# A graph-attention kernel: no summed table in its prologue, copies dealt to two more engines, and a last stage that adds on TensorE

## The chip, the cores and the metric

One NeuronCore of a Trainium2 chip runs the whole kernel. The metric is the device time of one execution in microseconds (us), less is better. Engines are named as in the profile: PE (TensorE, matrix products), DVE (VectorE), ACT (ScalarE), POOL (GpSimd) and SP (the engine that issues most transfers).

## The reference

One layer of graph attention over N = 6250 nodes with 256 features, 206,250 edges sorted by destination, 8 heads of 16 channels.

```
h    = relu(layernorm(x))
xm   = h @ W_n2m.T;  ea = edge_attr @ W_r2m.T
xl   = xm @ Wl.T + bl;  xr = xm @ Wr.T + br
# each node also gets a loop edge whose attribute is the mean of ea over its edges
u      = leaky_relu(xl[src] + xr[dst] + ea @ We.T, 0.2)
logits = sum over the 16 channels of a head of u * att
alpha  = softmax of logits over the edges of one destination
out    = segment_sum(xl[src] * alpha, dst) + bias
result = x + out @ W_m2n.T
```

## The kernel before

Nodes are cut into 49 windows of 128. The kernel has three stages, one function each, with a barrier between them; nothing of a stage overlaps the next.

**`prologue`** loads x, builds the index tables and masks, multiplies the weight matrices together, and then runs the **projection loop** over the 49 windows. In it, for window w: ACT writes `h` (the normalised and clipped x, L411); PE transposes it in two halves (L483, L484); DVE copies the transpose to `hT` (L647); PE forms `[xl | xr]` in two accumulated products with `Wall` (L490, L491); DVE adds the biases into `lr_sb` (L653). `xr` is then split into three bf16 parts whose sum is the float32 value, kept in `xr_parts`: ACT rounds it (L416), DVE forms the remainder `rest` (L658), ACT rounds that (L421), DVE stores the last remainder (L663). The steps of one window are spread over four turns of the loop. ACT, PE, DVE, POOL and SP each have an instruction list of their own, written out by hand; semaphores tie them. Each of xl and xr carries 8 extra columns (`ROW` = 136), the share of each head's logit that is linear in it (0.2 times the sum with `att`), so the product is 272 columns wide. POOL adds the two halves into `both` (L361) and SP stores it as `both_table` (L308) beside `xl_table` (L306). The extra columns of the weights come from `Watt`, `Wshare` and the copies L606 to L625, and PE spreads the bias row by a product (L473) ahead of the loop.

**`edge_loop`** walks the edges in 427 steps of 512: gathers xl rows by POOL's indirect transfers, adds xl, xr (through `xr_parts` and a one-hot matrix) and edge terms on PE, and gathers weighted sums into `acc`.

**`finale`** goes over the windows in 7 batches of `FB` = 7. For batch n: DVE takes `mean` of the edge attributes; PE transposes it (L1188), ACT copies it to `meanT` (32 rows, L1218), PE multiplies it with `Wc` (L1195); DVE adds `both_in`, loaded from `both_table`, giving `z` (L1290), takes `u_att` = max(z, 0) * att (L1292), sums it per head and adds the 8 linear columns for the loop edge's logit. For the batch b before it: DVE scales the gathered sums and the node's own xl by their weights (`old` L1268, `own` L1273), adds them (`two`, L1279), divides (`gat`, L1284); PE transposes `gat` (L1201), ACT copies it to `gatT` (L1221), PE multiplies it with `W_outT` in two groups of 4 and 3 windows through one buffer (L1209), ACT copies each to `result` (L1230), POOL adds x (L1175), SP stores. Each engine takes batch n = b + 1 and batch b in the same turn. The order on DVE in a turn is: means of n, everything of b up to `gat`, then `z` of n up to the softmax differences `falls`.

Of the kernel before, what the change touches and what calls it, by code (L numbers as in the profile page):

```python
# [24 lines left out]
ROW = D_MSG + HEADS  # L25
# [91 lines left out]
def gat_kernel(nc, x, src, dst, edge_attr, W_n2m, W_r2m, Wl, bl, Wr, br, We, att, bias, W_m2n, out):  # L117
# [6 lines left out]
    both_table = nc.dram_tensor("both_table", (WINDOWS * P, ROW), FP32, kind="Internal").ap()  # L124
# [4 lines left out]
    with ExitStack() as ctx:  # L129
        def sb(name, shape, dt=FP32):  # L130
# [8 lines left out]
        att_relu = sb("att_relu", [P, D_MSG])  # L139
        att_pad = sb("att_pad", [P, 2 * ROWS - HEADS])  # L140
        Wc = sb("Wc", [P, ROW])
# [12 lines left out]
                 both_table, xr_parts, ident, ident16, ones, iota_n, node_of, att_relu, att_pad, Wc, Wc2, W_outT,  # L154
# [6 lines left out]
        finale(nc, banks, x, xl_table, both_table, ident, att_relu, Wc, W_outT, bias_col, acc, out)  # L161


def prologue(nc, banks, xl_table, meta_dram, slot_dram, masks_dram, inputs,
             both_table, xr_parts, ident, ident16, ones, iota_n, node_of, att_relu, att_pad, Wc, Wc2, W_outT,
# [6 lines left out]
    with ExitStack() as ctx:  # L172
# [3 lines left out]
        def sem(name):  # L176
# [3 lines left out]
        lr_sb = sb("lr_sb", [P, WRING, 2 * ROW])  # L180
        lr_bias = sb("lr_bias", [P, 2 * ROW])
        rest = sb("rest", [P, WRING, D_MSG])
        both = sb("both", [P, WRING, ROW])
# [35 lines left out]


        Wall = sb("Wall", [P, 7, ROW])
        att_bc = sb("att_bc", [P, D_MSG])
        Watt = sb("Watt", [P, 7, D_MSG])
        Wshare = sb("Wshare", [P, 7, HEADS])
# [20 lines left out]
        ident16_ready, bias_spread, bias_ready = map(sem, ("ident16_ready", "bias_spread", "bias_ready"))  # L245
        wT_done, wT_ready, w_prod, w_copied, w_att, w_sum, w_share, w_ready = map(
            sem, ("wT_done", "wT_ready", "w_prod", "w_copied", "w_att", "w_sum", "w_share", "w_ready"))
# [12 lines left out]
        h_ready, hT_done, hT_ready, proj_done, lr_ready, both_ready, hi_ready, rest_ready, mid_ready, lo_ready = map(  # L260
            sem, ("h_ready", "hT_done", "hT_ready", "proj_done", "lr_ready", "both_ready", "hi_ready", "rest_ready",
                  "mid_ready", "lo_ready"))
# [14 lines left out]
        def _(sp):  # L277
# [26 lines left out]
            for w, s, _ in sweep(sp, 0, WRING, WINDOWS, WINDOWS, WRING, WRING):  # L304
                sp.wait_ge(lr_ready, w + 1)
                sp.dma_start(xl_table[bass.DynSlice(w * P, P), :], lr_sb[:, s, 0:D_MSG]).then_inc(lr_out[s], 16)  # L306
                sp.wait_ge(both_ready, w + 1)
                sp.dma_start(both_table[bass.DynSlice(w * P, P), :], both[:, s]).then_inc(lr_out[s], 16)  # L308
# [5 lines left out]
            for s in range(WRING):  # L314
                sp.wait_ge(lr_out[s], 32 * (-(-(WINDOWS - s) // WRING)))

        @block.gpsimd
        def _(pool):
# [37 lines left out]
            for w, s, r in sweep(pool, 0, WRING, WINDOWS, WINDOWS, WRING, WRING):  # L356

                pool.wait_ge(lr_ready, w + 1)
                if inside(w - WRING, WINDOWS):
                    pool.wait_ge(lr_out[s], r * 32)  # L360
                nc.gpsimd.tensor_tensor(both[:, s], lr_sb[:, s, 0:ROW], lr_sb[:, s, ROW:], ALU.add  # L361
                                        ).then_inc(both_ready, 1)

        @block.scalar
        def _(act):
# [40 lines left out]
            for w, s, _ in sweep(act, -2, WRING, WINDOWS - 2, WINDOWS + 2, WRING, WRING):  # L406
# [6 lines left out]
                if inside(w - 1, WINDOWS):  # L413

                    act.wait_ge(lr_ready, w)
                    nc.scalar.activation(parts_of(xr_parts, w - 1, 0), lr_sb[:, (s - 1) % WRING, ROW:ROW + D_MSG], ACT.Copy  # L416
                                         ).then_inc(hi_ready, 1)
                if inside(w - 2, WINDOWS):

                    act.wait_ge(rest_ready, w - 1)  # L420
                    nc.scalar.activation(parts_of(xr_parts, w - 2, 1), rest[:, (s - 2) % WRING], ACT.Copy  # L421
                                         ).then_inc(mid_ready, 1)

        @block.tensor
        def _(pe):
# [25 lines left out]
            for c in range(2):  # L451
                for i in range(2):
# [5 lines left out]
                             ).then_inc(w_prod, 1)  # L458

            for c, r in enumerate(chunk_rows):  # L460
# [10 lines left out]
            pe.wait_ge(w_share, 1)  # L471
            w_of = Wall[:].rearrange("p b r -> p (b r)")
            nc.tensor.matmul(wps[1][:, 0:2 * ROW], ones[0:1, :], w_of[0:1, 4 * ROW:6 * ROW], start=True, stop=True  # L473
                             ).then_inc(bias_spread, 1)
            pe.wait_ge(tab_copied, 2 * CHUNKS)
            for w, s, _ in sweep(pe, -1, WRING, WINDOWS - 2, WINDOWS, WRING, WRING):
# [8 lines left out]
                if inside(w, WINDOWS):  # L485
# [3 lines left out]
                    lr = proj_ps[s % 2][:, 0:2 * ROW]  # L489
                    nc.tensor.matmul(lr, hT[:, s % 2, 0:P], w_of[:, 0:2 * ROW], start=True, stop=False)  # L490
                    nc.tensor.matmul(lr, hT[:, s % 2, P:2 * P], w_of[:, 2 * ROW:4 * ROW], start=False, stop=True  # L491
# [3 lines left out]
        def _(dve):  # L495
# [108 lines left out]
            dve.wait_ge(w_prod, 6)  # L604
            nc.vector.memset(Wall[:, 4:6], 0.0).then_inc(w_copied, 1)
            nc.vector.tensor_copy(Wall[:, 0:4, 0:D_MSG], wps[0][:, 0:4 * P].rearrange("p (b d) -> p b d", b=4)  # L606
                                  ).then_inc(w_copied, 1)
            nc.vector.tensor_copy(Wall[:, 6, 0:D_MSG], wps[1][:, 0:D_MSG]).then_inc(w_copied, 1)
# [33 lines left out]
            for w, s, r in sweep(dve, -1, WRING, WINDOWS - 2, WINDOWS + 2, WRING, WRING):  # L642
                if inside(w + 1, WINDOWS):
                    dve.wait_ge(hT_done, w + 2)
                    if inside(w - 1, WINDOWS):
                        dve.wait_ge(proj_done, w)
# [417 lines left out]
def finale(nc, banks, x, xl_table, both_table, ident, att_relu, Wc, W_outT, bias_col, acc, out):  # L1064


    with ExitStack() as ctx:
# [50 lines left out]
        def span(tile, b):  # L1118
            return tile[:, bass.DynSlice(b * FB, FB)]
# [206 lines left out]
```

## Time and profile before

| | |
|---|---|
| median of 3 runs | 2524.55 us (2521.17 to 2527.56) |
| the profiled execution | 2522.38 us, of which the span from first to last instruction 2520.6 us |
| projection loop | first `lr_sb` at 103.6, last at 170.1 us |
| edge loop | about 175 to 2404.6 us |
| last stage | 2404.6 to 2520.6 us |
| busy over the span | PE 2279.6 us (90%), POOL 1709.8, DVE 1570.0, ACT 1424.5 |

Read it by stages: the busy shares of the whole are those of the edge loop. A stage's limit is seen in its own rows, in which engine has no idle time, and in whether its instructions take longer than the same ones elsewhere.

### The profile page before, as it was taken

Reading aid. Unit: us, or ns where it says so; the run is one execution under the profiler, and the core shown is the slowest. Engines: PE = TensorE matmul, PEld = TensorE weight load, DVE = VectorE, ACT = ScalarE, POOL = GpSimd, SP = SyncE. Lnnn points to the kernel's source line nnn. Section 1 sums busy time; section 2 is a strip of 40 time slices with the busy share of each in tenths; the row PEclk is TensorE's granted clock in tenths of the full one; section 3 lists DMA queues with packets and bytes.
Section 4 is the critical chain, followed back from the end, with each engine's and each line's share of the span. In section 5 each row is a group of like instructions: output and inputs, shape, how many; then the busy total and the mean of one; then the engine's idle time right before and its main releaser. Section 6 shows DMA issues by size and latency. Waiting matters only on the chain. (4 is left out here: it accounts for less than half of the span.)

```text
span 2520.6 us, 70463 instructions
## 1 busy us (share of the span) xinstructions
PE 2279.6 (90%) x16472; PEld 1731.7 (69%) x16473; DVE 1570.0 (62%) x4350; ACT 1424.5 (57%) x4365; POOL 1709.8 (68%) x1801
## 2 busy tenths in 40 slices
PE   2477899999999999999999999999999999999865
PEld 1355677776777777777767776777777777777654
DVE  4773566565666666656665665666566656666676
ACT  1351566565666566656665665666566656666722
POOL 1137777777777777777777777777777777777014
PEclk9988999999999999999999999999999999999977
DMA  6135344444444444434443444444444444443055
GB/s 192 61 96 118 84 99 99 96 99 96 99 97 100 94 99 98 98 96 98 98 99 94 99 100 95 99 98 99 94 100 99 98 97 98 99 98 95 6 151 158
DMA packets 306917, 251.64 MB, mean 100 GB/s; under 512 B 169239, under 2 KB 278264, under 8 KB 306482
## 3 DMA queue, kind: packets, MB, share of 16 engines
q1 hardware_dynamic: 246110, 128.97, 21.5%
q0 software_dynamic: 55232, 114.70, 18.7%
q10 hardware_dynamic: 5140, 3.04, 0.5%
q8 instruction: 167, 2.74, 0.4%
q14 instruction: 268, 2.20, 0.3%
HBM read 231.64 MB, written 17.31 MB: 99 GB/s over the span
## 5 line engine op out<-in xcount | busy, mean ns | idle before, releaser
L787 POOL DMA_INDIRECT xl_g<-xl_table,src_tab x1708 | 1637.8, 959 | 526.9 <-issue 517.4
L1005 DVE SCALAR_TENSOR_TENSOR uT<-banks,relu 128x256 f32<-128x256 f32 x854 | 349.3, 423 | 497.1 <-issue 469.1
L868 PE MATMUL banks<-msg,onehot 128*128 128x177 f32 x3416 | 631.4, 327 | 8.0 <-DVE acc L984 4.5
L868 PEld LDWEIGHTS banks<-msg,onehot 128*128 128x128 f32 x3416 | 515.8, 190 | 171.1 <-issue 168.8
L918 ACT ACTIVATE relu<-banks 128x256 f32<-128x256 f32 x854 | 319.5, 382 | 513.8 <-PE banks L813 460.8
L906 ACT ACTIVATE distance<-iota_n,minus_slot 128x128 f32<-128x128 f32 x1708 | 541.2, 392 | 0.5
L813 PE MATMUL banks<-ident,xl_g 128*128 128x128 f32 x3416 | 504.0, 291 | 19.3 <-DMA xl_g<-xl_table,src_tab 19.2
L984 DVE TENSOR_TENSOR acc<-acc,banks 128x177 f32 x854 | 289.4, 339 | 326.7 <-PE banks L868 224.5
L813 PEld LDWEIGHTS banks<-ident,xl_g 128*128 128x128 f32 x3416 | 421.7, 194 | 73.3 <-DMA xl_g<-xl_table,src_tab 23.1
L803 PE MATMUL banks<-onehotT,xr_parts 128*128 128x256 bf16 x2562 | 358.3, 277 | 32.7 <-issue 20.8
L911 ACT ACTIVATE onehot<-distance 128x512 f32<-128x512 f32 x427 | 268.9, 630 | 105.7 <-PE banks L868 93.8
L809 PE MATMUL banks<-rbfT,Wc 64*128 64x128 f32 x3416 | 310.6, 301 | 0.0
L803 PEld LDWEIGHTS banks<-onehotT,xr_parts 128*128 x2562 | 246.5, 98 | 87.4 <-issue 43.7
L995 DVE TENSOR_TENSOR msg<-xl_g,banks 128x512 f32<-128x512 f32 x427 | 291.7, 683 | 4.4 <-PE banks L879 2.5
L809 PEld LDWEIGHTS banks<-rbfT,Wc 64*128 64x128 f32 x3416 | 227.8, 189 | 90.5 <-issue 88.9
L852 PE MATMUL banks<-uT,att_pad 128*64 128x256 f32 x1708 | 282.7, 410 | 0.0
L960 DVE TENSOR_SCALAR onehotT<-slot_bc,node_of 128x512 bf16<-128x512 bf16 x427 | 161.9, 379 | 26.9 <-issue 19.1
L823 PE MATMUL banks<-ident,rbf 128*128 128x128 f32 x427 | 119.5, 280 | 51.4 <-DVE acc L984 43.8
L852 PEld LDWEIGHTS banks<-uT,att_pad 128*64 128x64 f32 x1708 | 85.4, 136 | 82.0 <-issue 54.3
L921 ACT ACTIVATE rbfT<-banks 128x128 f32<-128x128 f32 x427 | 116.5, 273 | 43.4 <-PE banks L823 43.4
L923 ACT ACTIVATE msg<-rbf 128x128 f32<-128x128 f32 x427 | 133.3, 312 | 0.0
L1175 POOL TENSOR_TENSOR result<-result,x_in 128x1024 f32<-128x1024 f32 (+1 forms) x14 | 35.8, 2569 | 141.9 <-ACT result L1230 141.6
(194 smaller groups left out, 1590.1 us busy)
## 6 DMA issues: line engine op xcount, KB each, us to landing
slot_bc<-slot_dram SPq DMA_DIRECT2D x427, 128.0 KB
rbf<-in_edge_attr SPq DMA_DIRECT2D x854, 32.0 KB
xl_g<-xl_table,src_tab POOLq DMA_INDIRECT x1708
masks<-masks_dram SPq DMA_DIRECT2D x864, 12.1 KB
x_sb<-in_x SPq DMA_DIRECT2D x6, 1024.0 KB, 16.2
x_in<-in_x SPq DMA_DIRECT2D x6, 896.0 KB, 8.0
out<-result SPq DMA_DIRECT2D x6, 896.0 KB, 5.1
both_table<-both SPq DMA_DIRECT2D x49, 68.0 KB, 1.6
```

What stands on the lines that cost most here:

```text
L787: pool.indirect_dma_start(out=xl_g[:, k % RING, t], out_offset=None, in_=xl_table, in_offset=bass.IndirectOffsetOnAxis(ap=src_tab[:, e:e + ...
L803: nc.tensor.matmul(z_ps[h], parts_of(xr_parts, w[h], part), onehotT[:, n4, h * PIECE:(h + 1) * PIECE], start=part == 0, stop=False)
L809: nc.tensor.matmul(z_ps[h][:, i::PT], Wc2[q, i], rbfT[q, n], start=False, stop=False)
L813: mm = nc.tensor.matmul(z_ps[h][:, i::PT], xl_g[:, s % RING, i * SPLIT + h], ident[:], start=False, stop=i == PT - 1)
L852: mm = nc.tensor.matmul(LT_ps[par][h * ROWS:(h + 1) * ROWS], att_pad[:, ROWS - HEADS - i * HEADS:2 * ROWS - HEADS - i * HEADS], uT[:, n, h ...
L868: mm = nc.tensor.matmul(U_ps[h], onehot[:, j % 2, t], msg[:, j % 2, t], start=i == 0, stop=i == PT - 1)
L906: nc.scalar.activation(distance[:, t], iota_n[:], ACT.Abs, bias=minus_slot[:, one(TILES * (k - LAG + 1) + t)]).then_inc(dist_ready, 1)
L911: nc.scalar.activation(onehot[:, m % 2], distance[:], ACT.Relu, scale=-1.0, bias=1.0).then_inc(oh_ready, TICK)
L918: nc.scalar.activation(relu[:, h], z_ps[h], ACT.Relu, scale=1.0 - SLOPE).then_inc(relu_ready, 2 + h)
L984: nc.vector.tensor_tensor(at(acc, w_sum[h]), at(acc, w_sum[h]), U_ps[h], ALU.add).then_inc(added, 1 + h)
L995: nc.vector.tensor_tensor(to[:, :, :, 0:D_HEAD], xl_g[:, m % RING].rearrange("p t (h d) -> p t h d", d=D_HEAD), w_ps[:, :, row].unsqueeze( ...
L1005: nc.vector.scalar_tensor_tensor(out=uT[:, s % 2, h * PIECE:(h + 1) * PIECE], in0=z_ps[h], scalar=SLOPE, in1=relu[:, h], op0=ALU.mult, op1 ...
```

## The change

It edits `prologue` and `finale`; `edge_loop` is the same text. In the prologue the 8 linear columns, `Watt`, `Wshare`, `both` and `both_table` are gone, so the product is 256 columns wide. The copy to `hT` is ACT's, and the two roundings into `xr_parts` are POOL's. In the last stage `z` is built on PE: the three bf16 parts of xr go in by products with a bf16 identity, 4 and 3 windows (512 and 384 columns) at a time, and the mean's product follows into the same banks, with `meanT` and `Wc` as full 128-row operands (rows 32 to 127 of `meanT` zero). DVE adds xl, ACT takes relu, DVE forms leaky relu from both (`u`), multiplies by `att` and sums. The weights are divided first (`shares`); `old` and `own` are then added by two accumulated products with the identity in place of one transpose. The output product fills 4 banks; DVE adds x to it straight from there (`results`), one batch later. The loops of the last stage are written out instead of looped by registers.

```diff
-                sp.dma_start(both_table[bass.DynSlice(w * P, P), :], both[:, s]).then_inc(lr_out[s], 16)
...
-                nc.gpsimd.tensor_tensor(both[:, s], lr_sb[:, s, 0:ROW], lr_sb[:, s, ROW:], ALU.add
-                                        ).then_inc(both_ready, 1)
+            for w, s, r in sweep(pool, 0, WRING, WINDOWS - 2, WINDOWS + 1, WRING, WRING):
+                if inside(w, WINDOWS):
+                    pool.wait_ge(lr_ready, w + 1)
+                    nc.gpsimd.tensor_copy(parts_of(xr_parts, w, 0), lr_sb[:, s, D_MSG:]).then_inc(hi_ready, 1)
+                if inside(w - 1, WINDOWS):
+                    pool.wait_ge(rest_ready, w)
+                    nc.gpsimd.tensor_copy(parts_of(xr_parts, w - 1, 1), rest[:, (s - 1) % WRING]).then_inc(mid_ready, 1)
...
+                if inside(w + 1, WINDOWS):
+                    act.wait_ge(hT_done, w + 2)
+                    if inside(w - 1, WINDOWS):
+                        act.wait_ge(proj_done, w)
+                    nc.scalar.activation(hT[:, (s + 1) % 2], hT_ps[(s + 1) % 2][:, 0:2 * P], ACT.Copy
+                                         ).then_inc(hT_ready, 1)
...
-            pe.wait_ge(w_share, 1)
+            pe.wait_ge(w_copied, 4)
...
-            nc.tensor.matmul(wps[1][:, 0:2 * ROW], ones[0:1, :], w_of[0:1, 4 * ROW:6 * ROW], start=True, stop=True
-                             ).then_inc(bias_spread, 1)
...
-            nc.vector.tensor_tensor(Watt[:], Wall[:, :, 0:D_MSG], att_bc[:].unsqueeze(1).broadcast_to([P, 7, D_MSG]),
-                                    ALU.mult).then_inc(w_att, 1)
...
-                    nc.vector.tensor_copy(hT[:, (s + 1) % 2], hT_ps[(s + 1) % 2][:, 0:2 * P]).then_inc(hT_ready, 1)
...
-                    nc.gpsimd.tensor_tensor(result[:, s, lo:hi], result[:, s, lo:hi], x_in[:, s, lo:hi], ALU.add
-                                            ).then_inc(result_ready, 1)
...
+                    if n:
                         pe.wait_ge(z_added, n)
+                    for lo, hi in halves:
+                        for part in range(PARTS):
+                            nc.tensor.matmul(z_ps[:, lo:hi], ident16[:], xr_parts[:, n * FB + lo:n * FB + hi, part],
+                                             start=part == 0, stop=False)
                     pe.wait_ge(meanT_ready, n + 1)
                     for i in range(FB):
-                        mm = nc.tensor.matmul(z_ps[:, i, 0:ROW], meanT[:, i], Wc[0:D_RBF, :],
-                                              start=True, stop=True)
+                        mm = nc.tensor.matmul(z_ps[:, i], meanT[:, i], Wc[:], start=False, stop=i + 1 in (4, FB))
...
-                        mm = nc.tensor.transpose(T_ps[:, i], gat[:, i], ident[:])
+                        nc.tensor.matmul(T_ps[:, i], old[:, b % 2, i], ident[:], start=True, stop=False)
+                        mm = nc.tensor.matmul(T_ps[:, i], own[:, b % 2, i], ident[:], start=False, stop=True)
                     mm.then_inc(gatT_done, 1)
                     pe.wait_ge(gatT_ready, b + 1)
...
+                    if b:
+                        pe.wait_ge(result_ready, 2 * b)
+                    for lo, hi in halves:
                         for i in range(lo, hi):
-                            mm = nc.tensor.matmul(y_ps[:, i - lo], gatT[:, i], W_outT[:], start=True, stop=True)
+                            mm = nc.tensor.matmul(y_ps[:, i], gatT[:, i], W_outT[:], start=True, stop=True)
...
+                    nc.scalar.activation(relu_z[:], z[:], ACT.Relu, scale=1.0 - SLOPE).then_inc(relu_done, 1)
...
+                    nc.vector.tensor_tensor(result[:, b % 2, lo:hi], y_ps[:, lo:hi], x_in[:, b % 2, lo:hi], ALU.add
+                                            ).then_inc(result_ready, 1)
```

In DVE's list ahead of the projection loop and in its first turns, before (names as in the section on the kernel before):

```order
L609 COPY att_bc<-banks 128x128
L610 TENSOR_SCALAR att_relu<-banks 128x128
L613 COPY Wall<-lr_row 1x2x128
L617 TENSOR_TENSOR Watt<-Wall,att_bc 128x896
L620 TENSOR_REDUCE Wshare<-Watt 128x56
L623 TENSOR_SCALAR Wall<-Wshare 128x7x8
L625 COPY Wc<-Wall 128x136
...
L647 COPY hT<-banks 128x256
L653 TENSOR_TENSOR lr_sb<-banks,lr_bias 128x272
L658 TENSOR_TENSOR rest<-lr_sb,xr_parts 128x128
L663 TENSOR_TENSOR xr_parts<-rest,xr_parts 128x128
```

and of the change:

```order
L590 COPY Wall<-banks 128x512
L591 COPY Wc<-banks 128x128
L592 COPY att_bc<-banks 128x128
L593 COPY lr_bias<-banks 128x256
...
L614 TENSOR_TENSOR lr_sb<-banks,lr_bias 128x256
L619 TENSOR_TENSOR rest<-lr_sb,xr_parts 128x128
L624 TENSOR_TENSOR xr_parts<-rest,xr_parts 128x128
```

Five instructions of DVE ahead of the loop and one of four in each turn of it are gone; the product L473 of PE, which waited for them, too.

In the last stage, one turn on DVE before (`falls` of the batch ahead of it stands first):

```order
L1306 TENSOR_TENSOR falls<-loop_logit,top 128x56
L1266 TENSOR_TENSOR total_old<-acc,weights 128x56
L1268 TENSOR_TENSOR old<-acc,weights 128x896
L1271 TENSOR_TENSOR total<-total_old,weights 128x56
L1273 TENSOR_TENSOR own<-xl_in,weights 128x896
L1276 RECIPROCAL inv_total<-total 128x56
L1279 TENSOR_TENSOR two<-old,own 128x896
L1284 TENSOR_TENSOR gat<-two,inv_total 128x896
```

and the same turn of the change, down to the logit of the next batch:

```order
L1225 TENSOR_TENSOR shares<-weights,inv_total 128x112
L1231 TENSOR_TENSOR old<-acc,shares 128x896
L1234 TENSOR_TENSOR own<-xl_in,shares 128x896
L1241 TENSOR_TENSOR z_loop<-banks,xl_in 128x896
L1209 TENSOR_TENSOR result<-banks,x_in 128x1024
L1209 TENSOR_TENSOR result<-banks,x_in 128x768
L1246 SCALAR_TENSOR_TENSOR u_loop<-z_loop,relu_z 128x896
L1249 TENSOR_TENSOR u_att_loop<-u_loop,att_bc 128x896
L1252 TENSOR_REDUCE loop_logit<-u_att_loop 128x56
```

Two large instructions (`two`, `gat`) have left DVE, three (two `result`, `u_loop`) have come.

One turn of the last stage on PE before:

```order
L1188 MATMUL banks<-ident,mean 32x128 x7
L1195 MATMUL banks<-Wc,meanT 128x136 x7
L1201 MATMUL banks<-ident,gat 128x128 x7
L1209 MATMUL banks<-W_outT,gatT 128x256 x7
```

and of the change:

```order
L1118 MATMUL banks<-ident,mean 32x128 x7
L1124 MATMUL banks<-xr_parts,ident 128x512 x3
L1124 MATMUL banks<-xr_parts,ident 128x384 x3
L1128 MATMUL banks<-Wc,meanT 128x128 x7
L1135 MATMUL banks<-ident,old 128x128
L1136 MATMUL banks<-ident,own 128x128
...
L1143 MATMUL banks<-W_outT,gatT 128x256 x7
```

The six wide products are new, and seven transposes have become fourteen products (seven pairs of L1135 and L1136).

## Rows read from the trace of the kernel before

**Rows 1.** The page: its first line.

```profile
span 2520.6 us, 70463 instructions
```

**Rows 2.** Busy time by stretch, last stage: us, busy by engine, PE's granted clock, DMA.

```profile
2404.60:2520.60 116.00, 70.55 (x294) 53.73 (x294) 85.52 (x133) 28.09 (x35) 36.12 (x15) 0.71 0.58 168
```

**Rows 3.** The instructions on lr_sb: duration min/median/max in ns, first and last start.

```profile
L653 DVE TENSOR_TENSOR lr_sb<-banks,lr_bias x49: 422/440/442, 103.6 to 170.1; 128x272 f32<-128x272 f32 x49
```

**Rows 4.** Groups by line, 108 to 170 us: busy us, mean ns, idle before.

```profile
L411 ACT ACTIVATE h<-x_sb,shift,rstd 128x256 f32 (+1 forms) x43 | 25.8, 599 | 2.8 <-issue 2.7
L663 DVE TENSOR_TENSOR xr_parts<-rest,xr_parts 128x128 f32 (+1 forms) x45 | 22.8, 506 | 0.0
...
L647 DVE COPY hT<-banks 128x256 f32<-128x256 f32 x45 | 18.5, 412 | 0.0
...
L658 DVE TENSOR_TENSOR rest<-lr_sb,xr_parts 128x128 f32<-128x128 f32 x45 | 12.5, 278 | 0.0
```

**Rows 5.** Timeline of PE in two early turns of the projection loop: start, us.

```profile
105.57 0.62 PE L490 MATMUL banks<-Wall,hT 128*128 128x272 f32 x2
...
106.71 0.62 PE L490 MATMUL banks<-Wall,hT 128*128 128x272 f32 x2
```

**Rows 6.** Timeline of POOL and DVE in one turn of the projection loop.

```profile
134.77 0.47 POOL L361 TENSOR_TENSOR both<-lr_sb 128x136 f32<-128x136 f32 x1 [0.91 <-DVE lr_sb L653]
134.81 0.57 DVE L663 TENSOR_TENSOR xr_parts<-rest,xr_parts 128x128 f32 x1
```

**Rows 7.** The one rounding copy that POOL makes, line 343.

```profile
L343 POOL CAST ident<-ident x1: 291/291/291, 4.6 to 4.6; 128x128 bf16<-128x128 f32 x1
```

**Rows 8.** Timeline ahead of the projection loop.

```profile
95.85 1.09 DVE L617 TENSOR_TENSOR Watt<-Wall,att_bc 128x896 f32<-128x896 f32 x1
...
98.36 1.27 PE L473 MATMUL banks<-Wall,ones 1*128 1x272 f32 x2 [30.80 <-DVE Wall L623]
```

**Rows 9.** Groups by line, last stage, 2437 to 2491 us.

```profile
L1175 POOL TENSOR_TENSOR result<-result,x_in 128x1024 f32<-128x1024 f32 (+1 forms) x8 | 20.9, 2622 | 34.3 <-ACT result L1230 34.1
...
L1284 DVE TENSOR_TENSOR gat<-two,inv_total 128x896 f32<-128x896 f32 x5 | 13.5, 2691 | 0.2
L1279 DVE TENSOR_TENSOR two<-old,own 128x896 f32<-128x896 f32 x4 | 9.8, 2455 | 0.0
...
L1268 DVE TENSOR_TENSOR old<-acc,weights 128x896 f32<-128x896 f32 x4 | 4.3, 1082 | 0.0
L1221 ACT ACTIVATE gatT<-banks,bias_col 128x896 f32<-128x896 f32 x4 | 4.0, 1007 | 18.8 <-PE banks L1201 18.8
```

**Rows 10.** Timeline of DVE: z of the first, the second and the last batch.

```profile
2412.01 1.15 DVE L1290 TENSOR_TENSOR z_loop<-banks,both_in 128x952 f32<-128x952 f32 x1 [6.30 <-PE banks L1195]
...
2423.55 1.15 DVE L1290 TENSOR_TENSOR z_loop<-banks,both_in 128x952 f32<-128x952 f32 x1 [1.59 <-PE banks L1195]
...
2490.98 1.15 DVE L1290 TENSOR_TENSOR z_loop<-banks,both_in 128x952 f32<-128x952 f32 x1 [1.02 <-PE banks L1195]
```

**Rows 11.** Timeline of PE in the edge loop at the full clock.

```profile
1200.61 0.82 PE L803 MATMUL banks<-onehotT,xr_parts 128*128 128x256 bf16 x6
1201.36 0.71 PE L809 MATMUL banks<-rbfT,Wc 64*128 64x128 f32 x8
1202.00 1.16 PE L813 MATMUL banks<-ident,xl_g 128*128 128x128 f32 x8
1203.00 0.27 PE L823 MATMUL banks<-ident,rbf 128*128 128x128 f32 x1
```

**Rows 12.** Busy time by stretch as in rows 2, three in a row.

```profile
2422.70:2429.50 6.80, 5.70 (x19) 4.37 (x18) 5.26 (x14) 1.30 (x2) 0.00 (x0) 0.50 0.01 2
2429.50:2436.30 6.80, 4.55 (x29) 3.42 (x27) 6.77 (x6) 2.69 (x3) 5.22 (x2) 1.00 0.00 0
2436.40:2443.10 6.70, 4.50 (x14) 3.57 (x15) 6.37 (x15) 1.30 (x2) 0.01 (x1) 0.50 0.86 252
```

**Rows 13.** Timeline of POOL: its last additions.

```profile
2509.59 4.17 POOL L1175 TENSOR_TENSOR result<-result,x_in 128x1024 f32<-128x1024 f32 x2 [5.42 <-ACT result L1230]
```

More of the change, by code:

```diff
@@ L24 @@
 STEPS = -(-(PIECES + WINDOWS - 1) // SPLIT)
-ROW = D_MSG + HEADS
 PARTS = 3
@@ L179, in prologue @@
         x_sb = sb("x_sb", [P, WINDOWS, D_NODE])
-        lr_sb = sb("lr_sb", [P, WRING, 2 * ROW])
-        lr_bias = sb("lr_bias", [P, 2 * ROW])
+        lr_sb = sb("lr_sb", [P, WRING, 2 * D_MSG])
+        lr_bias = sb("lr_bias", [P, 2 * D_MSG])
         rest = sb("rest", [P, WRING, D_MSG])
-        both = sb("both", [P, WRING, ROW])
         pads = sb("pads", [META_ROWS - PIECES, 3, PIECE], I32)
@@ L218, in prologue @@
         Wout = sb("Wout", [P, 2, D_MSG])
[L221 to L224, printed above, removed]
+        Wall = sb("Wall", [P, 4, D_MSG])
         lr_row = sb("lr_row", [1, 2 * D_MSG])
@@ L458, in _ @@
                              ).then_inc(w_prod, 1)
+            nc.tensor.matmul(wps[1][:, 2 * D_MSG:4 * D_MSG], ones[0:1, :], lr_row[:], start=True, stop=True
+                             ).then_inc(w_prod, 1)
             for c, r in enumerate(chunk_rows):
@@ L1088, in finale @@
         weights = sb("weights", [P, 2, FB, HEADS])
-        old = sb("old", [P, FB, D_MSG])
-        own = sb("own", [P, FB, D_MSG])
-        z = sb("z_loop", [P, FB, ROW])
-        two = sb("two", [P, FB, D_MSG])
-        gat = sb("gat", [P, FB, D_MSG])
         total_old = sb("total_old", [P, FB, HEADS])
@@ L1265, in _ @@
+            for b in range(-1, FBATCH):
+                n = b + 1
+                if n < FBATCH:
+                    means(n)
+                if b >= 0:
                     dve.wait_ge(weights_done, b + 1)
-                    nc.vector.tensor_tensor(total_old[:], sums[:, :, :, D_HEAD], weights[:, 0], ALU.mult
+                    nc.vector.tensor_tensor(total_old[:], sums_of(b)[:, :, :, D_HEAD], weights[:, 0], ALU.mult
                                             ).then_inc(told_done, 1)
-                    nc.vector.tensor_tensor(heads(old[:]), sums[:, :, :, 0:D_HEAD], spread(weights[:, 0]), ALU.mult
-                                            ).then_inc(old_done, 1)
@@ L1278, in _ @@
-                    dve.wait_ge(own_done, b + 1)
-                    nc.vector.tensor_tensor(two[:], old[:], own[:], ALU.add).then_inc(two_done, 1)
-                    dve.wait_ge(two_done, b + 1)
                     dve.wait_ge(itotal_done, b + 1)
-                    if inside(b - 1, FBATCH):
-                        dve.wait_ge(gatT_done, b)
-                    nc.vector.tensor_tensor(heads(gat[:]), heads(two[:]), spread(inv_total[:]), ALU.mult
-                                            ).then_inc(gat_done, 1)
```

295 lines of the change are left out of this document (131 added, 164 removed).

## The prediction

> **What bounds the kernel now.** I read the page first, then busy time by stretch, then groups by line and the timelines in the two stages that the change touches. The span is 2520.6 us [rows 1]. The stages follow each other behind barriers, so a microsecond taken from the end of one moves all that follows. The edge loop, nearly nine tenths of it, keeps its text, and I cost it at nothing: no instruction, transfer or buffer size of it differs, only addresses.
>
> The projection loop runs from 103.6 to 170.1 us for 49 windows [rows 3], 66.5/48 = 1.385 us each. DVE's four instructions in a turn are busy 0.412 + 0.44 + 0.278 + 0.506 = 1.64 us [rows 3, 4], more than the turn (their ends overlap), and none of them has idle time before it: DVE is the bound. PE could do a turn in 106.71 - 105.57 = 1.14 us, seen before DVE had all four [rows 5]. Note also the last subtraction, 506 ns on average, against 278 for one of the same size [rows 4]: it waits while POOL adds. In one turn POOL's starts at 134.77 and DVE's, 0.04 us later, takes 0.57 [rows 6].
>
> The last stage lasts 116.0 us, with PE's granted clock at 0.71 on average and DVE busy 85.5 [rows 2]. From the second z to the seventh it takes (2490.98 - 2423.55)/5 = 13.49 us a batch [rows 10]. `two` and `gat` take 2.46 and 2.69 us there, `old` of the same size 1.08 [rows 9]; POOL's additions of 2.6 us stand over them. DVE is the bound again, and 3.0 us of its turn are this wait.
>
> **Part 1, ahead of the projection loop.** PE's first work there waits for DVE's column sums until 98.36, and is itself a product of 1.27 us that goes; `Watt` alone takes 1.09 us [rows 8], and `Wshare` reads as many elements. Without these and three small ones, PE can start about when `Watt` did, some 95.6: 4.0 us sooner than 98.36 + 1.27. The copy to `hT` no longer stands behind DVE's small instructions, which gives 0.8 more, but PE starts slow there and part of that is lost. I take **4.0 us**; at least 2.5 (PE's product and `Watt` with it), at most 5.
>
> **Part 2, the projection loop.** DVE loses `hT`: 0.44 + 0.278 + 0.278 busy, 1.0 us and less with overlap, if POOL leaves it alone. ACT has 0.60 for `h` [rows 4] and a copy about as long as DVE's 0.41 for `hT`: 1.0. POOL has two copies of 0.29 [rows 7]. So PE is next: 1.14 us less 16 of 272 columns, 1.09. The engines also lose time at the loop's branch every fourth turn: 2.7 us over 43 turns before `h` [rows 4], 0.06 each. That makes 1.15; I add 0.03 for turns in which POOL holds DVE back too long. With 1.18 us and 45 turns at that rhythm: 45 x (1.385 - 1.18) = **9.2 us**. Bounds: 1.09 gives 13.3. From the other side, POOL's copies can each hold back one subtraction of DVE as its addition does now. Two such waits of 0.29 on 0.33 + 0.20 + 0.20 (the starts of DVE's instructions lie some 0.08 closer than their durations) are 1.31 us, a gain of 3.4. The store of `both` goes beside it; SP was not waited for, nothing. What waits on POOL: `rest` of a window needs its first copy, but one turn later, so a chain is no closer than a whole turn.
>
> The trace shows that the two block each other for the whole of an instruction [rows 6]. By the Trainium skill (SBUF — State Buffer, Who interferes with whom) a DVE instruction with two inputs in SBUF and a GpSimd one that reads SBUF take an exclusive lock in order of issue; both subtractions have two such inputs, and the rule then speaks against dealing the copies to POOL. By it the sum would be that of the upper period.
>
> **Part 3, the last stage, DVE.** Take 13.49 us a batch. Out: the waits of `two` and `gat` and both instructions, 2.46 + 2.69; z narrower, 0.06. In: `u` with 1.1, and two `result` of 1024 and 768 elements, by z's 1.15 for 952 about 1.2 and 0.95. Small ones even out, and the register work of the loop, some 0.2, goes: 13.49 - 5.15 - 0.06 + 3.25 - 0.2 = 11.3. ACT's relu of z, about 1.0, lies under `result`, except in the first two batches, which have none: 1.0 each.
>
> **Part 4, the last stage, PE.** Prices at the full clock from starts in the edge loop [rows 11]: a float32 pass of 128 columns 0.125 us (eight from 1202.00 to 1203.00), six bf16 products of 256 columns 0.75 (1200.61 to 1201.36). Wider passes go by their columns: four of 272 and two of 128 make 1.14 us in the projection loop [rows 5], 0.85 ns a column. Per batch: seven mean transposes 0.8; parts, 2688 bf16 columns, 1.15; mean product 14 passes 1.75; `old` and `own` 28 passes 3.5, where 7 single passes were; output product 14 passes of 256, 3.05 and the end of the last one, 3.2. Sum 10.4, and between them a wait for ACT's `gatT` of 1.01 [rows 9], with both hand-overs 1.3. PE's round is 11.7 us and just longer than DVE's; they also wait for each other (z for 3.8 us of PE after the mean, with 3.6 of DVE beside it). I take 11.75. ACT's copy of `meanT` is hidden by the parts.
>
> At the low clock, 0.50 in the first and third of the three stretches [rows 12], the passes take twice as long. In the first batch PE then needs 7.4 us where it needed 6.3, so z comes 1.1 later, at 2413.1. The second waits as well: 6.0 of DVE, then 7.4 of PE and 0.8 between, 14.2 us where 11.5 were. From the second z to the third, with PE finishing the output of batch 0, 12.8. Then four of 11.75. First to seventh z: 74.0, against 2490.98 - 2412.01 = 79.0. After the last z, 29.6 us now. Then: z 1.1, results 2.1, u to falls 3.85, exp and means of weights 1.65, `old` and `own` 2.1, PE 3.5, ACT 1.3, output 3.4, last addition 0.95, and from the end of POOL's last one at 2513.8 to the end 6.8 [rows 13]: 26.7. I add 1.5 for PE falling to the low clock in the gap: 28.2. The stage gives +1.1 - 5.0 - 1.4 = **-5.3 us**. Bounds: -10 (the clock rises one batch sooner, DVE's 11.3 binds, no fall at the end), and +12, the third case below.
>
> **Sum.** -4.0 - 9.2 - 5.3 = -18.5 us on the profiled execution of 2522.4, which gives 2503.9. That execution lies 2.2 under the median shown; on the median it is 2506.0.
>
> **Rivals.**
> 1. POOL and DVE take turns in the projection loop, 1.31 us a window: 5.8 less gain, **2512**. For it: the 506 ns of now. Against: POOL's copies are shorter than its addition, and PE's 1.09 leaves DVE room.
> 2. PE's clock in the last stage goes on changing between its levels. Now it rises behind a stretch in which PE, at the low level, was busy 5.70 of 6.80 us, most of it the products of `gatT`, and falls behind one with 4.55 busy, largely mean transposes and 32-row products [rows 12]. The change turns both kinds into full-height products and fills 10.4 of 11.75 us, so I expect it to stay up. If it alternates, PE's round is 10.4/0.75 + 1.3 = 15.1 us, and the stage is 12 us longer than now: -13.2 + 12, **2523**.
> 3. The slower side, one mechanism: PE stays at the low clock through the last stage, and the doubled products make a round of 20.8 + 1.3 = 22 us. 2427.3 for the second z, five rounds, 33 to the end: 50 us longer, **2561**. It decides from a round of 15.3 us on (no gain), 16.8 for slower by over 0.3%. Against it: at that clock PE would hardly idle, and behind less work than that it rose [rows 12].
> 4. The sums do not add up as moved: the two stages gain, and the edge loop, of 2230 us, runs differently with its buffers elsewhere. 0.6% of it, 13 us, would hide the gain, 21 would turn it. Nothing in the trace speaks for it but that 0.3% is what runs of one kernel differ by.
>
> **The numbers.** The forecast as worked out (2498 to 2510) 0.53; gain larger by the better bounds (about 2496 to 2498) 0.08; rival 1, 0.18; rival 2, 0.12; rival 3, 0.03; rival 4, 0.06. About 0.3%, 7.6 us, is what a measurement of this kernel tells from no change, so faster is under 2517. The first three cases are: 0.79, and a little of rival 4 and of rival 2 with a mixed clock, 0.81. Same 0.12, slower 0.07. The range takes in rival 1 and most mixtures of clocks: 2496 to 2519.
>
> **What would show it.** Projection loop: `lr_sb` starts 1.15 to 1.2 us apart, DVE with idle time before it that ends on PE, its last subtraction near 280 ns; if that stays near 500 and DVE has no idle time, rival 1. First `lr_sb` near 99. Edge loop: 2230 us from barrier to barrier, as now. Last stage: z of batches 2 to 6 about 11.75 us apart, granted clock 1.00 from the second batch on, no DVE instruction of 896 elements over 1.2 us, PE with little idle time but before the output product. Wrong would be z to z above 13 us with the clock at 0.50 in it, DVE idle before z for more than 1 us in each batch, or an edge loop that moved by more than 5 us.

## The result, and the profile after

The changed kernel takes 2508.27 us in the median of 5 runs (2505.85 to 2511.58), the kernel before 2527.56 in 5 (2521.17 to 2529.06): a ratio of 0.9931, with a 95% interval of 0.9915 to 0.9947. By the ratio that is faster by 17 us, by the medians by 19. The profiled execution took 2507.61 us. By its spans the gain is 2520.6 - 2505.8 = 14.8 us. The forecast was 2506.0, from a gain of 18.5 us on the 2524.55 known then. The total came out nearly as forecast; the parts did not.

The first line of the page (to [rows 1]), the busy time of the last stage (to [rows 2]), and where the edge loop begins (DVE's one memset of `msg`) and ends (its first `deg`):

```profile
span 2505.8 us, 70476 instructions
```

```profile
2388.30:2505.80 117.50, 76.63 (x483) 63.31 (x483) 78.27 (x140) 21.46 (x28) 0.84 (x1) 0.93 0.46 137
```

```profile
L902 DVE MEMSET msg<- x1: 65/65/65, 154.0 to 154.0; 128x8 f32 x1
L1186 DVE TENSOR_SCALAR deg<-acc x7: 162/164/823, 2388.3 to 2471.2; 128x7 f32<-128x7 f32 x7
```

Before, the same two stood at 174.7 and 2404.7 us. So the account, in us:

| | before | after | difference | forecast |
|---|---|---|---|---|
| up to the edge loop | 174.7 | 154.0 | -20.8 | -13.2 |
| edge loop | 2230.0 | 2234.4 | +4.4 | 0 |
| last stage | 115.9 | 117.5 | +1.6 | -5.3 |

**Projection loop.** The instructions on `lr_sb` (to [rows 3]), groups by line from 108 to 149 us (to [rows 4]) and one turn on PE (to [rows 5]):

```profile
L614 DVE TENSOR_TENSOR lr_sb<-banks,lr_bias x49: 423/425/426, 97.8 to 150.4; 128x256 f32<-128x256 f32 x49
```

```profile
L614 DVE TENSOR_TENSOR lr_sb<-banks,lr_bias 128x256 f32<-128x256 f32 x38 | 16.1, 425 | 9.5 <-PE banks L476 8.9
...
L348 POOL CAST xr_parts<-lr_sb 128x128 f32 x36 | 13.8, 382 | 16.6 <-DVE lr_sb L614 16.6
...
L351 POOL CAST xr_parts<-rest 128x128 f32 x36 | 10.5, 292 | 0.0
...
L624 DVE TENSOR_TENSOR xr_parts<-rest,xr_parts 128x128 f32 x36 | 10.2, 284 | 0.0
```

```profile
120.25 0.60 PE L475 MATMUL banks<-Wall,hT 128*128 128x256 f32 x2
...
121.33 0.60 PE L475 MATMUL banks<-Wall,hT 128*128 128x256 f32 x2
```

A window takes (150.4 - 97.8)/48 = 1.096 us, the time that PE needs (121.33 - 120.25 = 1.08). DVE waits for PE, its last subtraction is back at 284 ns. POOL's casts and DVE's subtractions overlap, and here it is the cast that gets longer, 382 ns against 291 alone [rows 7], not the subtraction (timelines of DVE and POOL):

```profile
121.85 0.29 DVE L624 TENSOR_TENSOR xr_parts<-rest,xr_parts 128x128 f32 x1
```

```profile
121.91 0.39 POOL L348 CAST xr_parts<-lr_sb 128x128 f32 x1 [0.27 <-DVE lr_sb L614]
```

**Last stage.** DVE's timeline, two rows of the third batch and the last z (to [rows 10]); ACT's and PE's beside it:

```profile
2421.32 1.09 DVE L1241 TENSOR_TENSOR z_loop<-banks,xl_in 128x896 f32<-128x896 f32 x1 [0.31 <-PE banks L1128]
2422.33 2.08 DVE L1209 TENSOR_TENSOR result<-banks,x_in 128x1024 f32<-128x1024 f32 x2
2426.39 1.09 DVE L1246 SCALAR_TENSOR_TENSOR u_loop<-z_loop,relu_z 128x896 f32<-128x896 f32 x1 [1.99 <-ACT relu_z L1164]
...
2476.25 1.09 DVE L1241 TENSOR_TENSOR z_loop<-banks,xl_in 128x896 f32<-128x896 f32 x1 [0.68 <-PE banks L1128]
```

```profile
2424.51 1.01 ACT L1159 ACTIVATE gatT<-banks,bias_col 128x896 f32<-128x896 f32 x1 [5.11 <-PE banks L1136]
2425.42 0.94 ACT L1164 ACTIVATE relu_z<-z_loop 128x896 f32<-128x896 f32 x1
```

```profile
2425.57 3.29 PE L1143 MATMUL banks<-W_outT,gatT 128*128 128x256 f32 x14 [1.10 <-ACT gatT L1159]
2431.16 0.94 PE L1118 MATMUL banks<-ident,mean 128*32 128x128 f32 x7 [2.29 <-DVE mean L1192]
```

`z` ends at 2422.4, but ACT's relu of it starts only at 2425.42: it stands in ACT's list behind the copy to `gatT`, which waits for PE's 14 products. DVE idles 1.99 us for it in each of four batches (3.91 in the second, 1.62 in the last), and PE then 2.29 us for DVE. From the third to the seventh z a batch takes (2476.25 - 2421.32)/4 = 13.73 us, where 11.75 were forecast. The clock did nearly as forecast (busy time by stretch, to [rows 12]): full from the second z on, low at the last products:

```profile
2421.30:2476.20 54.90, 41.33 (x281) 34.72 (x281) 44.15 (x80) 12.20 (x16) 0.00 (x0) 1.00 0.58 168
2488.80:2491.50 2.70, 2.64 (x12) 2.67 (x13) 1.96 (x2) 0.00 (x0) 0.00 (x0) 0.50 0.00 0
```

### The profile page after: what moved, and what is told of

It reads as the page before. It is cut to its first block and busy times, and to the rows that moved or that the text cites. A ratio compares the mean times of both kernels' runs of the same rounds, so it can differ in the third digit from the quotient of the medians.

```text
span 2505.8 us, 70476 instructions
## 1 busy us (share of the span) xinstructions
PE 2276.5 (91%) x16661; PEld 1744.0 (70%) x16662; DVE 1530.6 (61%) x4301; ACT 1409.9 (56%) x4309; POOL 1680.5 (67%) x1836
## 5 line engine op out<-in xcount | busy, mean ns | idle before, releaser
L784 PEld LDWEIGHTS banks<-ident,rbf 128*128 128x128 f32 x427 | 61.8, 145 | 63.0 <-issue 63.0
```

## The experiments

Each kernel starts from the changed one, unless it is said. Lengths of stages are read from the same two instructions as above. TensorE's clock at the start of the last stage differs from trace to trace (the first seven mean transposes take 0.94 to 1.68 us), and the first z comes 5.2 to 8.1 us behind that start. Where its text is the same (the changed kernel twice, runs 4, 5 and 6) the stage took 117.5, 117.5, 117.8, 119.2 and 119.2 us, so a difference of under 2 us between two traces of it tells nothing.

**1. The relu first.** In ACT's list, last stage:

```
+                relu_z of n (waits for z_added, u_done)
                 gatT of b (waits for gatT_done, y_done)
-                relu_z of n (waits for z_added, u_done)
```

> The changed kernel with one edit: in ACT's list of the last stage the relu of batch n stands before the copy to gatT of batch b, not behind it. Theory (ACT's order is what costs): in the changed kernel DVE idles 3.91 us in the second batch and 1.99 in each of the five after it before u_loop, because that relu stood behind a copy that waits for PE's 14 products. That idle time goes to under 0.3 us, z to z falls from 13.64 to about 11.7 us (DVE's own work 11.3, PE's about 11.6), the stage from 117.5 to about 106 us, the kernel to about 2497 us. Rival (PE's round binds anyway): the idle time only moves from before u_loop to before z_loop, z to z stays above 13 us, and the kernel stays within 2 us of 2508.

Measured: ratio 0.9908 (0.9891 to 0.9924), stage 111.5 us. The idle time before `u_loop` is gone from the third batch on. But from the second z to the seventh it is (2470.95 - 2406.28)/5 = 12.93 us, not 11.7. DVE's and SP's timelines in the fourth and fifth batch (SP's rows are transfers issued), and PE's output product behind that z:

```profile
2432.83 1.08 DVE L1246 SCALAR_TENSOR_TENSOR u_loop<-z_loop,relu_z 128x896 f32<-128x896 f32 x1
...
2443.98 1.09 DVE L1241 TENSOR_TENSOR z_loop<-banks,xl_in 128x896 f32<-128x896 f32 x1 [2.89 <-issue]
```

```profile
2432.94 0.38 SPq L1097 DMA_DIRECT2D out<-result  x1
2433.37 0.57 SPq L1083 DMA_DIRECT2D x_in<-in_x  x1
2433.98 1.34 SPq L1094 DMA_DIRECT2D xl_in<-xl_table  x1
```

```profile
2447.21 4.95 PE L1143 MATMUL banks<-W_outT,gatT 128*128 128x256 f32 x14 [2.66 <-DVE result L1209]
```

The order on ACT is shown as the cause of the 1.99 us. Behind it stood a second limit that neither theory had: z also needs `xl_in`, and its transfer is issued behind the store of `out` and the load of x. The one issued at 2433.98 landed 9.9 us later, at 2443.9, and z began at 2443.98. The late z made PE wait as well, and behind that wait its clock fell: the 14 output products took 4.95 us, not 3.29.

**2. The transfer of xl sooner.** Run 1 and, in SP's list:

```
+                xl of b + 3 (waits for own of b + 1)
                 wait for results of b; store out; load x of b + 2
-                xl of b + 3, at the start of the next turn
```

> The kernel of the run with the relu first, and one edit more, in SP's list: the transfer of the next xl (448 KB) stands ahead of the wait for results, so that it is issued before the store of out and the load of x (896 KB each) and not behind them. In that run z of the last batches waited 2.89, 1.56 and 2.92 us for nothing that the trace names; SP had issued out, x and then xl at 2432.9, 2433.4 and 2434.0, and z came at 2444.0. Theory (that wait was the transfer of xl): no idle time of that kind is left before z, z to z from the second to the seventh falls from 12.93 to 11.7 to 12 us (PE's round), the stage from 111.5 to about 106 us, the kernel to 0.988 to 0.989 of the kernel before. Rival (the 16 DMA engines are full: 2.24 MB a batch at the 350 GB/s seen at most take 6.6 us, at the mean of 138 GB/s 16 us): the wait moves to result, for x or for the store, and z to z stays near 12.9.

Measured: ratio 0.9888 (0.9872 to 0.9904), stage 104.8 us. The fifth and sixth z:

```profile
2437.73 1.09 DVE L1243 TENSOR_TENSOR z_loop<-banks,xl_in 128x896 f32<-128x896 f32 x1 [0.31 <-PE banks L1130]
...
2449.29 1.09 DVE L1243 TENSOR_TENSOR z_loop<-banks,xl_in 128x896 f32<-128x896 f32 x1 [0.31 <-PE banks L1130]
```

and PE's mean transposes between them:

```profile
2445.49 0.94 PE L1120 MATMUL banks<-ident,mean 128*32 128x128 f32 x7 [0.21 <-DVE mean L1194]
```

11.56 us a batch, with 0.31 idle on DVE. The wait was the transfer's: from issue to landing it now takes 4.1 us in the median, where run 1 had 8.2. DVE's own work is 11.25 us, where Part 3 of the prediction had 11.3. But DVE alone is not the bound. PE idles 0.21 for DVE's means and DVE 0.31 for PE's mean products, in every batch: the round goes through both. Against the changed kernel in the same rounds (next run) this is 2493.2 to 2506.1 us, 12.9 less for two instructions moved.

**3. The changed kernel again**, unedited.

> The changed kernel once more, unedited, timed in the same rounds as the run with xl sooner. It gives their ratio, and a further length of the edge loop. So far its text ran in 2230.0, 2234.4, 2233.2, 2230.5, 2231.2 and 2236.5 us. Theory (chance): another value between 2229 and 2237, the last stage 117.5 within 0.5, the projection loop 1.096 us a window. Rival (the changed kernel's own): 2234.4 within 0.5.

Measured: ratio 0.9928 (0.9914 to 0.9942), last stage 117.5, projection loop 1.110 us a window, edge loop 2235.1 us. The edge loop in all 13 traces, in the order in which they were taken: 2230.0 (before), 2234.4 (after), 2233.2, 2230.5, 2231.2, 2236.5, 2232.1, 2235.1, 2227.0, 2233.2, 2232.6, 2226.1, 2230.1. Kernels whose prologue and buffers are those of the changed one lie between 2230.1 and 2235.1, those with the prologue of before at 2230.0, 2227.0 and 2236.5. The two traces of the changed kernel are 0.7 apart, so the traces alone leave open whether a length belongs to the kernel or to the execution. The whole times say more: without any edit, the kernel before ran in 2517.7 to 2529.1 us and the changed one in 2502.2 to 2511.6. The 4.4 us are within that.

**4. The prologue of before with the new last stage.**

> The prologue of the kernel before (with the summed table, the linear columns and the old dealing) together with the last stage of the changed kernel. If the stages add up: first memset of the edge loop at about 174.7 us as before, last stage 117.5 us as in the changed kernel. The edge loop tells whether its 2234 us against 2230 has to do with where buffers lie: with that theory it comes out at 2230 here, since the prologue's buffers and tables are those of before, and the kernel at about 2524; if it is the last stage's or chance, anything from 2229 to 2235.

One run, 2529.7 us. The edge loop began at 173.2 us, the last stage took 117.8: the stages do add up, and the new last stage alone gains nothing (115.9 us before). The edge loop took 2236.5 us, the longest of all: the prologue's buffers and tables of before do not bring 2230 back.

**5. The dealing undone.** `hT` copied by DVE, both roundings by ACT, nothing on POOL.

> The changed kernel with the dealing undone in the projection loop: the copy to hT on DVE and both roundings on ACT as before; the 256 columns and the missing table stay, so POOL does nothing there. Theory A (two halves: POOL's addition cost DVE 0.23 us a window, the copy the rest): DVE's 0.41 + 0.40 + 0.28 + 0.28 less some overlap gives 1.2 us a window against 1.096 in the changed kernel and 1.385 before, so the prologue is about 5 us longer than in the changed kernel, the kernel about 2513. Theory B (the dealing is all of the gain): 1.38 us a window, 14 us longer, 2522. In both the last subtraction is near 280 ns, if it was POOL that lengthened it.

Measured: ratio 0.9945 (0.9928 to 0.9962). The instructions on `lr_sb`, and the group of the last subtraction:

```profile
L616 DVE TENSOR_TENSOR lr_sb<-banks,lr_bias x49: 412/423/426, 98.6 to 158.9; 128x256 f32<-128x256 f32 x49
```

```profile
L626 DVE TENSOR_TENSOR xr_parts<-rest,xr_parts 128x128 f32 x33 | 9.4, 283 | 0.0
```

1.256 us a window, and the edge loop begins 8.5 us later than in the changed kernel: between the two theories, nearer A. Of 0.289 us gained in a window, 0.129 come without the dealing and 0.160 by it.

**6. POOL's addition back.** Run 5 and:

```
+                nc.gpsimd.tensor_tensor(both[:, s], lr_sb[:, s, 0:D_MSG], lr_sb[:, s, D_MSG:], ALU.add)
```

> The changed kernel with the dealing undone (1.256 us a window) and POOL's addition back in the projection loop: 128 columns of xl and xr into a buffer that is not stored. Theory (POOL's two-input addition holds DVE's subtraction back, and that was on the path): the last subtraction goes from 283 to about 500 ns, a window takes 1.35 to 1.4 us, the loop 5 to 6 us longer. Rival (the 16 columns less and the missing store made the difference between 1.385 and 1.256): the window stays under 1.30 us, with the subtraction at either length.

```profile
L623 DVE TENSOR_TENSOR lr_sb<-banks,lr_bias x49: 406/409/426, 98.3 to 165.9; 128x256 f32<-128x256 f32 x49
```

```profile
L633 DVE TENSOR_TENSOR xr_parts<-rest,xr_parts 128x128 f32 x29 | 16.3, 563 | 0.0
L349 POOL TENSOR_TENSOR both<-lr_sb 128x128 f32<-128x128 f32 x29 | 13.2, 455 | 28.0 <-DVE lr_sb L623 28.0
```

1.408 us a window, slower than before the change (1.385) with 16 columns less and no store. The addition lengthens the subtraction from 283 to 563 ns and costs 0.15 us of every window, 7.3 us in all. So the part of the gain that came without the dealing is POOL's addition, not the narrower product.

The Trainium skill (SBUF — State Buffer, Who interferes with whom) has this rule, that a DVE instruction with both inputs in SBUF and a GpSimd one that reads SBUF shut each other out, and that the order of issue decides who waits; the traces agree on both. Here POOL's addition starts first (121.53, DVE's subtraction at 121.57), and the subtraction takes 563 ns, not 283. In the changed kernel the subtraction starts first (121.85, POOL's cast at 121.91), and the cast is the longer one.

**7. Before, without POOL's addition of x** in the last stage: it covers 8 of 256 columns, and the rest of x is missing from the result.

> The kernel before with POOL's addition of x in the last stage cut to 8 of 256 columns (the rest of x is left out of the result); all waits stay. Theory A (the prediction's: DVE bounds that stage, and 3.0 us of its turn are the wait for POOL's port): two and gat take 1.1 us each, z to z falls from 13.49 to about 10.6 us, the stage from 116 to about 100 us. Theory B (PE at its changing clock bounds it, or soon after DVE does): two and gat take 1.1 us, but DVE idles before z for longer, and z to z stays above 12 us; the stage gains less than 10 us.

```profile
2455.99 1.03 DVE L1279 TENSOR_TENSOR two<-old,own 128x896 f32<-128x896 f32 x1
2457.06 1.09 DVE L1284 TENSOR_TENSOR gat<-two,inv_total 128x896 f32<-128x896 f32 x1
2460.62 1.15 DVE L1290 TENSOR_TENSOR z_loop<-banks,both_in 128x952 f32<-128x952 f32 x1 [2.47 <-PE banks L1195]
```

```profile
2418.20:2487.90 69.70, 52.90 (x211) 38.93 (x212) 48.78 (x96) 20.12 (x25) 4.75 (x11) 0.67 0.59 168
```

Theory B. `two` and `gat` lost their 3.0 us of waiting, and z to z did not fall: (2487.86 - 2418.16)/5 = 13.94 us against 13.49. From the third z on DVE idles 2.5 to 4.6 us before each for PE, whose clock was 0.67 on average (0.75 in the kernel before). The stage still gained 4.3 us: 2.1 before the first z and 4.5 behind the last, less 2.3 lost between them. The 2.1 are not the edit's: none of the edited instructions has run by then, and the clock was 0.96 in that stretch where it had been 0.56. The 4.5 are: POOL's last additions had taken 4.17 us [rows 13]. So in the kernel before, PE at its changing clock was as near a bound as DVE, and the wait for POOL cost nothing in the batches by itself.

**8. The mean's product over 32 rows again.**

```
-                nc.tensor.matmul(z_ps[:, i], meanT[:, i], Wc[:], start=False, ...)
+                nc.tensor.matmul(z_ps[:, i], meanT[0:D_RBF, i], Wc[0:D_RBF, :], start=False, ...)
```

> The changed kernel with the mean's product over 32 rows again (meanT and Wc cut to their 32 filled rows), nothing else. Theory (the padding to 128 rows is what keeps TensorE's clock up): the granted clock falls to 0.50 again in the stretch of mean transposes and mean products of each batch, z to z rises from 13.64 to 15 us or more, the kernel to 2515 or more. Rival (PE is filled by the parts and the 14 products, the padding does nothing): granted clock 1.00 from the second batch on, z to z 13.6, the kernel within 2 us of 2508.

One run, 2506.06 us; the batches from the third z to the seventh:

```profile
2417.90:2473.30 55.40, 41.84 (x277) 34.48 (x278) 44.12 (x80) 12.20 (x16) 0.00 (x0) 1.00 0.58 167
```

Granted clock 1.00 throughout, 13.86 us a batch. So the zero rows of the mean's product are not what keeps the clock up.

**9. `old` and `own` added on DVE**, 7 transposes on PE in place of the 14 products.

> The changed kernel with old and own added on DVE (in place, 896 elements) and 7 transposes on PE as before, in place of the 14 products. By the theory of ACT's order: gatT is ready 2 us sooner, so the relu behind it too, and DVE's idle time of 1.99 us before u_loop goes (3.91 in the second batch mostly), while DVE has 1.1 us more to do: z to z 12.7 us, the stage 117.5 - 8 = about 110 us, faster than the changed kernel. It also asks what holds the clock up: PE is then busy some 8.7 of 12.7 us. Theory (filled time): the granted clock falls to 0.50 in part of the batches, as it does before the change, and z to z is 13 us or more. Rival: 1.00 from the second batch on.

One run, 2500.27 us. The batches together, and three stretches of one of them:

```profile
2417.70:2470.40 52.70, 37.31 (x199) 28.88 (x199) 48.23 (x85) 12.60 (x17) 0.00 (x0) 0.90 0.61 175
2430.00:2434.00 4.00, 0.98 (x7) 0.75 (x7) 3.05 (x4) 1.95 (x2) 0.00 (x0) 1.00 0.02 5
2434.00:2438.00 4.00, 3.61 (x11) 2.98 (x12) 3.86 (x7) 0.00 (x0) 0.00 (x0) 0.67 0.69 192
```

Stage 112.7 us against 117.5: undoing this part of the change gained 4.8 us, since `gatT` and the relu behind it come sooner. The clock is no longer full: 0.90 over the batches, and 0.67 just behind a stretch in which PE was busy 0.98 of 4.00 us. So the 14 products help to keep it up, by the time that they fill. They are not enough by themselves: in run 1 they stood in every batch, and the clock fell all the same behind a wait of 2.66 us. z to z was 12.95 us, since `xl_in` came late here too (up to 1.40 us).

**10. The same on top of run 2.**

> The kernel with relu first and xl sooner, with old and own added on DVE again and 7 transposes on PE. Theory (with ACT's order and the transfer in place DVE bounds that kernel: 11.56 us a batch with 0.31 idle): DVE's 1.09 us more make z to z 12.5 to 12.7 us, the stage about 6 us longer than its 104.8, whatever PE saves; so the 14 products are worth their place on PE only once ACT's order is right. Rival (PE's round was the bound and its 1.6 us less carry it): z to z stays near 11.6.

```profile
2442.44 1.08 DVE L1244 TENSOR_TENSOR z_loop<-banks,xl_in 128x896 f32<-128x896 f32 x1
...
2454.81 1.08 DVE L1244 TENSOR_TENSOR z_loop<-banks,xl_in 128x896 f32<-128x896 f32 x1
```

One run, 2497.25 us: 12.37 us a batch with no idle time before z, so here DVE alone is the bound (11.25 and 1.09 more), stage 109.4 against 104.8. PE's clock was 0.93 on average in these batches, and that cost nothing there. Once ACT's order and the transfer are right, the sum belongs on PE. By itself in the changed kernel it cost more than it gave.

**11. Gaps filled.** Run 2 and, on PE, products that nobody reads:

```
+                    if n == 0:
+                        for i in range(24):
+                            nc.tensor.matmul(y_ps[:, 0, 0:P], ident[:], ident[:], start=True, stop=True)
...
+                if b == FBATCH - 1:
+                    for i in range(12):
+                        nc.tensor.matmul(z_ps[:, 0], ident[:], ident[:], start=True, stop=True)
```

> The kernel with relu first and xl sooner, and products of the identity with itself, whose results nobody reads, in two gaps of PE in the last stage: 24 behind the first batch's mean product (PE idle 6.91 us there) and 12 ahead of the last batch's products (idle some 3 us). Theory (PE falls to the low clock because it idles there, and comes back late): granted clock 1.00 through both gaps, the second z 11.0 us behind the first and not 12.9, the last 14 products 3.1 us and not 6.1, the stage 104.8 - 5 = about 100 us, the kernel about 0.986 to 0.987 of the kernel before. Rival (the clock falls by itself, or products of that kind do not hold it): 0.50 in the same places, the stage 105 us or longer by what the fillers delay.

PE's timeline in the first gap, and busy time by stretch over all batches:

```profile
2390.48 5.52 PE L1134 MATMUL banks<-ident 128*128 128x128 f32 x48
2397.56 0.94 PE L1120 MATMUL banks<-ident,mean 128*32 128x128 f32 x7 [1.55 <-DVE mean L1201]
```

```profile
2390.60:2484.00 93.40, 75.99 (x529) 65.42 (x527) 76.22 (x135) 21.22 (x27) 0.00 (x0) 0.99 0.51 154
```

Ratio 0.9874 (0.9852 to 0.9896), stage 101.5 us. The second z comes 10.68 us behind the first (12.91 in run 2, 11.8 to 13.3 in the other changed kernels without the fillers), and the end 26.5 us behind the last z (29.3 in run 2, 28.1 at the least in those others). The second batch's mean transposes take 0.94 us; in all 12 traces without the fillers they take 1.67 or 1.68. By the traces this beats run 2 by 3.3 us of stage, and by 4.9 behind the first z: that z came 1.5 us sooner in run 2, with the clock full at the stage's start. The intervals of the two kernels' times overlap.

## Why the prediction came out as it did

**Part 1 held, with a shift from elsewhere.** The first `lr_sb` came 5.8 us sooner. 1.0 of that was there before any changed instruction (`shift` started at 93.87 before and 92.91 after); the rest, 4.8, lies in the range of 2.5 to 5 (with the same prologue of before it came at 102.5 and 102.1 us in runs 7 and 4, so 1 to 1.5 us of this is noise). PE's first transposes began at 94.50, at once behind the copy to `lr_bias`.

**Part 2: mechanism right, size off.** PE did become the bound, POOL did not hold DVE back. Rival 1, by which POOL's copies hold back two subtractions, fell by the order of issue: the subtraction starts 0.06 us ahead of the cast, which then waits itself, and POOL has time to spare. The mis-sized term is the step from PE's 1.09 us to 1.18: 0.06 for the loop's branch and 0.03 for POOL. Neither is there; 1.096 us were measured. The branch's time was read from idle time of ACT [rows 4], and ACT is not the bound after the change. With 48 windows instead of 45, the loop gave 13.9 us where 9.2 were forecast, and 1.0 more came at its end. Run 6 shows what the prediction only inferred from 506 ns: POOL's addition was on the path.

**Parts 3 and 4: the sums of the engines were right, the order between them was missed.** DVE's turn was put at 11.3 us and is 11.25 (run 2); PE's round was put at 11.7 and is 11.35 there, 11.56 less 0.21 idle. That the two wait for each other was in Part 4 too. The step that failed is the sentence that ACT's relu of z "lies under `result`, except in the first two batches". It took the relu's 1.0 us as a duration to be hidden, and did not look at what stands ahead of it in ACT's list: a copy that waits for the 14 products. The relu ends 3.9 us after z does, and `result` covers 2.0. The prediction asked of other added waits who is queued behind them, not of this one. The Trainium skill (TensorE: Matmul & The Clock Gate, Architectural detail: the array is 16× 32×32, not 1× 128×128) says that ACT takes its instructions strictly in order, and the trace agrees: relu at 2425.42, `gatT` at 2424.51, although z had been there since 2422.4. It cost 3.9 us in the second batch, where 1.0 had been allowed, 2.0 in each of the next four, and 1.6 behind the last z. Stretch by stretch, in us:

| | forecast | measured | difference |
|---|---|---|---|
| start of the stage to the first z | 8.5 | 6.6 | -1.9 |
| first to second z | 14.2 | 12.8 | -1.4 |
| second to third | 12.8 | 13.6 | +0.8 |
| third to seventh | 47.0 | 54.9 | +7.9 |
| last z to the end | 28.2 | 29.6 | +1.4 |

The sum is 6.8 us worse; the 6.9 between -5.3 and +1.6 differs from it by rounding. With the relu first, the end came 28.15 us behind the last z (run 1), as forecast.

Part 3 also took 3.0 us a batch as gained by the end of the wait for POOL, and called DVE the bound. Run 7 shows that removing this wait alone gains nothing from z to z in the kernel before, since PE was as late. The gain needed the clock too, and both came with the change: that the sum for DVE's turn fits is in part luck, since the prediction did not work out PE's round of before. That the transfer of xl would be the next limit (run 1) was in neither the prediction nor the first theory.

**The clock, rival 2.** It stayed full from the second z on, as forecast, for half of the reason given: the zero rows of the mean's product do nothing (run 8), filled time does (runs 9 and 11). That no rival came true does not mean that the forecast's working did: the prologue was 7.6 us better, the last stage 6.9 worse, and the edge loop 4.4 longer, with nothing to tell it from chance. That the total came within 2.3 us of the forecast is in good part luck: the misses have opposite signs. None of the three signs named for "wrong" was met in full: z to z was above 13 us, but at the full clock, and DVE idled over 1 us, but before `u_loop` and not before z. They were drawn for the failures that had been thought of. Open is why one edge loop differs from the next by up to 10 us; nothing was tried on it.

## What to carry to other kernels

Where an added instruction is said to be hidden, look at the list of the engine that runs it: what stands ahead of it, what that waits for, and only then how long it takes itself. When one wait is removed, the next is often on a transfer: check where in the issuing engine's list the load stands, and put a small load that is needed first ahead of large ones (runs 1 and 2). Here an engine's turn summed from the rows of instructions of the same size held within a few per cent (11.3 for 11.25 us, 11.7 for 11.35); what failed was the claim that two such turns run beside each other.

## What the runs showed of the hardware beyond what was expected

- POOL's two-input addition doubled a DVE subtraction of 128 columns (283 to 563 ns), but its one-input casts left it at 284 ns and were lengthened themselves (291 to 382 ns); in each case the one that started later, by 0.04 to 0.06 us, was the longer.
- TensorE's clock is held by products whose results nobody reads: with 5.5 us of them in a gap of 6.9, the work behind the gap ran at full clock (transposes 0.94 us, not the 1.67 or 1.68 of all 12 other traces), and a stage of 105 us became 3.3 us shorter.
- The clock fell behind short waits too: in run 1 behind 2.66 us, with PE busy 12.0 of the 14.2 us of the batch ahead of it.
- The same edge loop took 2226.1 to 2236.5 us in 13 traces, 0.5%, with no edit that reached it. A difference of 4 us between two profiled executions of this kernel tells nothing by itself. The last stage of the changed kernel agreed within 0.1 us in its two traces, but the same text took up to 119.2 us behind another prologue.
